# The moving operands of an LSTM's products widened from 8 to 56 columns in the recurrent stage of an eight-part kernel

## What is computed

```
# L2_cond: an LSTM over time; h is (8, 128), Wh is (128, 512)
z = xz_t + prev_h @ Wh
i, f, o = sigmoid(z's first three quarters);  g = tanh(z's last quarter)
next_c = f * prev_c + i * g
next_h = o * tanh(next_c)

# L2_attn: a delta rule, state S (8 batches, 8 heads, 32, 32), on silu(LSTM output @ W_in)
kn = k / (norm(k) + 1e-06)
retrieved = einsum('bhij,bhj->bhi', S, kn)
S = tanh(beta[..., None] * S + (v - retrieved)[..., None] * kn[..., None, :])
Sq = einsum('bhij,bhj->bhi', S, q);  out = Sq * silu(Sq);  x = x + out @ W_out

# L2_cond2: a plain recurrence on the new x
next_h = tanh(prev_h @ Wh + xw_t)
```

## Time and profile before

| | |
|---|---|
| median of 3 runs | 3087.18 us (3081.48 to 3088.09) |
| span of the profiled execution | 3083.1 us |
| mean granted TensorE clock | 0.683 of full speed |
| TensorE (matmul) busy | 86% |
| VectorE / ScalarE / GpSimd busy | 56% / 36% / 24% |

### The profile page before, as it was taken

One profiled execution on the slowest core, in us unless ns is written; L12 is line 12 of the kernel. 1 busy time (PEld: TensorE's weight loads), 2 busy tenths in 40 slices (PEclk: granted clock), 3 DMA queues, 4 the chain that ended last, 5 costly groups with the idle time before them and its releaser, 6 DMA issues. The chain is left out here.

```text
span 3083.1 us, 91254 instructions
## 1 busy us (share of the span) xinstructions
PE 2640.3 (86%) x36709; PEld 1928.4 (63%) x36714; DVE 1738.8 (56%) x7330; ACT 1114.5 (36%) x3986; POOL 750.8 (24%) x1223
## 2 busy tenths in 40 slices
PE   5998878873898889679999999999965878999998
PEld 3556666662555566456777777777543546677774
DVE  3544555555454544456666666666434775576675
ACT  1332333332232223234444444444435433333332
POOL 2110000001110000155555565565523320000000
PEclk9995555555898789555555555555555995799999
DMA  2000000000000000154354455445310000000000
GB/s 86 3 2 2 2 2 3 2 2 37 2 3 1 0 1 0 69 109 85 73 105 86 70 92 91 80 80 105 79 41 1 2 1 2 2 3 2 3 3 15
DMA packets 223764, 103.88 MB, mean 34 GB/s; under 512 B 89472, under 2 KB 220544, under 8 KB 222464
## 3 DMA queue, kind: packets, MB, share of 16 engines
q1 hardware_dynamic: 223360, 98.23, 15.5%
HBM read 89.81 MB, written 8.39 MB: 32 GB/s over the span
## 5 line engine op out<-in xcount | busy, mean ns | idle before, releaser
L641 POOL TENSOR_TENSOR l2r_beta_s<-l2r_state,l2r_beta_f 128x256 f32<-128x256 f32 x512 | 365.9, 736 | 392.3 <-ACT l2r_state L548 374.0
L548 ACT ACTIVATE l2r_state<-l2r_pre 128x256 f32<-128x256 f32 x512 | 191.6, 417 | 267.8 <-DVE l2r_pre L796 267.8
L796 DVE TENSOR_TENSOR l2r_pre<-l2r_o_ps,l2r_beta_s 128x256 f32<-128x256 f32 x512 | 193.7, 420 | 70.8 <-PE l2r_o_ps L439 39.6
L439 PE MATMUL l2r_o_ps<-l2r_rows,l2r_outer 32*128 32x128 f32 x2048 | 207.8, 497 | 13.5 <-DVE l2r_rows L788 13.5
L140 PE MATMUL l0r_bank<-main_x,l0r_wx_half 128*128 128x32 f32 (+2 forms) x480 | 147.4, 407 | 60.5 <-ACT l0r_out_gate L196 60.0
L427 PE MATMUL l2r_d_ps<-l2r_state,l2r_kq 128*32 128x128 f32 x2056 | 176.2, 421 | 13.7 <-ACT l2r_state L548 13.2
L140 PEld LDWEIGHTS l0r_bank<-main_x,l0r_wx_half 128*128 128x128 f32 x480 | 116.2, 304 | 81.7 <-ACT l0r_out_gate L196 79.5
L788 DVE TENSOR_TENSOR l2r_rows<-l2r_d_ps,main_even_layers 128x128 f32<-128x128 f32 x257 | 75.0, 292 | 153.1 <-PE l2r_d_ps L427 151.2
L1785 PEld LDWEIGHTS l3r_bank<-main_x,l3r_wx_half 128*128 128x128 f32 x480 | 96.6, 228 | 90.9 <-issue 46.3
L439 PEld LDWEIGHTS l2r_o_ps<-l2r_rows,l2r_outer 32*128 32x128 f32 x2048 | 132.4, 307 | 33.5 <-DVE l2r_rows L788 28.0
L194 ACT ACTIVATE l0r_gates<-l0r_bank 128x24 f32<-128x24 f32 x256 | 48.9, 191 | 234.4 <-PE l0r_bank L152 234.4
(11 more groups left out here) (582 smaller groups left out, 7320.4 us busy)
## 6 DMA issues: line engine op xcount, KB each, us to landing
l2r_beta_f<-l2r_beta_store SPq DMA_DIRECT2D x256, 256.0 KB, 7.2
main_odd_layers<-in_l SPq DMA_DIRECT2D x1, 4826.5 KB, 15.3
main_odd_layers<-in_l SPq DMA_DIRECT2D x1, 3672.0 KB, 16.4
l2r_v_store<-l2r_v_part SPq DMA_DIRECT2D x32, 96.0 KB, 3.4
l2r_v_rows<-l2r_v_store SPq DMA_DIRECT2D x16, 192.0 KB, 3.2
main_decay<-in_decay SPq DMA_DIRECT2D x1, 3072.0 KB, 10.2
main_even_layers<-in_l SPq DMA_DIRECT2D x1, 2762.5 KB, 10.4
l2r_beta_store<-l2r_beta_tok SPq DMA_DIRECT2D x64, 32.0 KB, 2.0
```

What stands on the lines that cost most here:

```text
L439: last = nc.tensor.matmul(o_ps[:, c, 0:P], outer[chunk_rows(c), n // TC % 2, n % TC, :, :].rearrange("p a b -> p (a b)"), rows[chunk_rows( ...
L548: nc.scalar.activation(state[:, h * 2 * P:(h + 1) * 2 * P], pre[:, h * 2 * P:(h + 1) * 2 * P], ACT.Tanh).then_inc(state_ready[h], 1)
L641: nc.gpsimd.tensor_tensor(beta_s[:, half].rearrange("p (c i) -> p c i", i=N2), state[:, half].rearrange("p (c i) -> p c i", i=N2), beta_f[ ...
L796: nc.vector.tensor_tensor(pre[:, half].rearrange("p (c n) -> p c n", c=2), o_ps[:, 2 * h:2 * h + 2, 0:P], beta_s[:, half].rearrange("p (c ...
```

## The change

The tiles that hold h and its parts become 56 columns wide where they were 8. The 48 new columns are set to zero once, at the stage's start, by four GpSimd memsets that stand before the memsets of `consts_ready`. Each of the 24 LSTM products of a step now moves all 56 columns, and writes 56 PSUM columns from its gate's place on; the 48 further ones get zeros added. The vector operations and the projection read and write the first 8 columns as before. No instruction is taken away or moved, and there is no new wait.

```
+WIDE = 7 * B
...
-        h_ring = mem.sb("h_ring", [P, SLOTS, B])
-        h_rest, h_mid, h_low = mem.sb("h_rest", [P, B]), mem.sb("h_mid", [P, B], BF16), mem.sb("h_low", [P, B], BF16)
+        h_ring = mem.sb("h_ring", [P, SLOTS, WIDE])
+        h_rest, h_mid, h_low = mem.sb("h_rest", [P, WIDE]), mem.sb("h_mid", [P, WIDE], BF16), mem.sb("h_low", [P, WIDE], BF16)
...
-                                last = nc.tensor.matmul(lstm_at(n, g, g + 1), w_part[k][:, g * P:(g + 1) * P],
+                                last = nc.tensor.matmul(lstm_at(n, g, g + WIDE // B), w_part[k][:, g * P:(g + 1) * P],
                                                         h_parts[m], start=False, stop=(m == 2), skip_group_check=True)
...
-                                         h_ring[:, w % 2 * TC:(w % 2 + 1) * TC, :].rearrange("p t b -> p b t"),
+                                         h_ring[:, w % 2 * TC:(w % 2 + 1) * TC, 0:B].rearrange("p t b -> p b t"),
...
+                nc.gpsimd.memset(h_ring[:, :, B:WIDE], 0.0)
+                nc.gpsimd.memset(h_rest[:, B:WIDE], 0.0)
+                nc.gpsimd.memset(h_mid[:, B:WIDE], 0.0)
+                nc.gpsimd.memset(h_low[:, B:WIDE], 0.0)
                 nc.gpsimd.memset(kn_rows[:, :, :], 0.0)
...
-                    nc.vector.tensor_tensor(h_ring[:, n % SLOTS, :], lstm_at(n, 2, 3), tanh_c[:, :],
+                    nc.vector.tensor_tensor(h_ring[:, n % SLOTS, 0:B], lstm_at(n, 2, 3), tanh_c[:, :],
                                             ALU.mult).then_inc(s["h_ready"], 1)
```

More of the change, by code:

```diff
@@ L759, in lstm_h @@
                         dve.wait_ge(s["xin_psum"], n // TC - 1)
-                    nc.vector.tensor_tensor(h_ring[:, n % SLOTS, :], lstm_at(n, 2, 3), tanh_c[:, :],
+                    nc.vector.tensor_tensor(h_ring[:, n % SLOTS, 0:B], lstm_at(n, 2, 3), tanh_c[:, :],
                                             ALU.mult).then_inc(s["h_ready"], 1)
                 def split_alone(n):
-                    h = h_ring[:, n % SLOTS, :]
+                    h = h_ring[:, n % SLOTS, 0:B]
                     dve.wait_ge(s["h_ready"], n + 2)
-                    nc.vector.tensor_tensor(h_rest[:, :], h, high(h), ALU.subtract).then_inc(s["rest_ready"], 1)
+                    nc.vector.tensor_tensor(h_rest[:, 0:B], h, high(h), ALU.subtract).then_inc(s["rest_ready"], 1)
                     dve.wait_ge(s["rest_ready"], n + 2)
-                    nc.vector.tensor_tensor(h_low[:, :], h_rest[:, :], high(h_rest[:, :]), ALU.subtract).then_inc(s["low_ready"], 1)
+                    nc.vector.tensor_tensor(h_low[:, 0:B], h_rest[:, 0:B], high(h_rest[:, 0:B]), ALU.subtract).then_inc(s["low_ready"], 1)
                 def split_h(n):
@@ L776, in split_h @@
                     dve.wait_ge(s["h_psum"], count)
-                    nc.vector.tensor_tensor(rest, lstm_at(n, 3, 4), high(h_ring[:, n % SLOTS, :]),
+                    nc.vector.tensor_tensor(rest, lstm_at(n, 3, 4), high(h_ring[:, n % SLOTS, 0:B]),
                                             ALU.subtract).then_inc(s["rest_psum"], 1)
                     dve.wait_ge(s["rest_psum"], count)
-                    nc.vector.tensor_copy(h_mid[:, :], high(rest)).then_inc(s["mid_h_ready"], 1)
+                    nc.vector.tensor_copy(h_mid[:, 0:B], high(rest)).then_inc(s["mid_h_ready"], 1)
                     dve.wait_ge(s["mid_h_ready"], count)
-                    nc.vector.tensor_tensor(h_low[:, :], rest, h_mid[:, :], ALU.subtract).then_inc(s["low_ready"], 1)
+                    nc.vector.tensor_tensor(h_low[:, 0:B], rest, h_mid[:, 0:B], ALU.subtract).then_inc(s["low_ready"], 1)
                 def masked(n):
@@ L860, in add_out @@
                                             ALU.add).then_inc(s["x_added"], 1)
-                nc.vector.tensor_copy(h_ring[:, SLOTS - 1, :], h0).then_inc(s["h_ready"], 1)
+                nc.vector.tensor_copy(h_ring[:, SLOTS - 1, 0:B], h0).then_inc(s["h_ready"], 1)
                 nc.vector.tensor_copy(r_ring[:, SLOTS - 1, :], h0).then_inc(s["r_ready"], 1)
```

## The result

The changed kernel takes 3171.28 us (median of 4 runs, 3140.52 to 3190.46), the kernel before 3086.8 us beside it: a ratio of 1.0253, 95% interval 1.0202 to 1.0303. It is slower by 2.5%; 2991 us had been forecast, in a range up to 3115. The ratio is taken without the slowest of the four runs, which lies more than 1.5% above the fastest.

The account below looks back on a forecast made before the run. TensorE's order was taken to bound the recurrent steps. -112 us for 224 steps (85% at full clock), +14 and +2 give -96: span 3083.1 becomes 2987, and with 4.1 added, 2991 us; range 2925 to 3115.

Parts of the forecast that it names:

- the forecast of the clock: Recurrent stage: full clock within a wave or two of body 2, for 85% of 224 steps; chance 0.52 for over 80%.
- rival (a): Clock flickers in the recurrent steps; half at full clock gives 3080 us; chance 0.22 still faster, 0.10 slower or near it.
- Rival (b): Clock does not rise, since zeros, or columns as such, don't count: +119 us, 3206 us; chance 0.16.
- The terms at the half clock: 24 widened products cost 0.46 us more a step, weight load hidden: +103 us over 224 steps if the clock stays.
- TensorE's order leaves no slack: In steady recurrent steps the products run straight into `retrieve`, so their whole 0.46 us is paid.
- Alone: The 31 steps where the LSTM runs without the delta rule: +0.46 us each, +14 us.
- Setup: Four new memsets at the stage's start, all on the path: +2 us.
- The term at the full clock: Recurrent steps with LSTM and delta rule: -0.67 us each, 3.03 instead of 3.70, bounds -0.45 and -0.80.
- VectorE is next: At the full clock VectorE's own order limits the recurrent step; nearly all of its 0.62 us waiting goes.
- theory A: Formed after the result: granted clock follows columns streamed through the whole array, zeros included; 56 fall just short.

Follow-up runs that it names:

- The kicked run: The changed kernel with 8 columns in steps 0 to 31 and 20 extra 384-column matmuls after the delta rule's first step: 3154.83 us, ratio 1.0210.
- real data: The changed kernel with the 48 further columns repeating the 8 real columns of h in place of zeros: 3158.62 us, ratio 1.0234.

## Why the prediction was wrong

**The step that failed** is the forecast of the clock: "I take it that the clock rises within a wave or two of body 2 and mostly stays", and in the sum "with 85% of the 224 steps at the full clock". In the profiled execution it was some 6%: 14 steps. That execution is the slowest. If the rest of the program had the full clock for as long in every run, the fastest run (0.707 of 3138.7 us, against 0.684 of 3188.6) had it for some 126 us more in this stage, beside the 48 read in the trace, which would be 20% (an estimate). By that none of the four comes near 85%.

The direction of the mechanism was right (more columns through the whole array do raise the clock: 0.57, 0.90, 0.95, 0.99 for 56, 64, 72, 88), but a step was only said to "come near to that mix" of l3r and, "in its steps with more pieces", to pass it. Near was not enough. And the comparison with l3r was made at the half clock alone. At the full clock an l3r step takes 1.72 us (L1797 starts at 2896.68 and again at 2898.40 in the kernel before), while a step of this stage still takes 3.1, because other engines hold it, so l3r gives TensorE more per microsecond there. Even so l3r lost the clock. The reading that the clock "stayed there" after 2916 leaves out that the same stage had been at 1.0 before 2905 and fell:

```profile
2826.00:2910.00 84.00, 81.72 (x1365) 64.68 (x1364) 57.24 (x319) 30.71 (x155) 1.59 (x3) 0.97 0.01 3
```

The kicked run and the later rises of all four kernels with 56 columns show the same: even at the full clock these steps don't keep it. It was rival (a), flicker, far on the slower side of the 47% at which it turns slower, and that side had a chance of 0.10. Rival (b), 3206 us, is near in time, but its cause is shown wrong: zeros count as data does.

**The terms at the half clock were right.** 0.46 us a step was forecast for the products; 4.18 - 3.70 = 0.48 was measured in three waves, and 0.46 over all 203 steps of the stretch that were at the half clock throughout (4.14, against 3.68 before), with 46.7 ns a product to the tenth and the weights' load hidden. That TensorE's order leaves no slack is shown by VectorE's wait, up by 0.35 us. Alone: 0.46 forecast, 2.5 against 2.0 measured, 13 us in all for the 14. Setup: the timeline of GpSimd in the changed kernel, which answers to the earlier trace rows,

```profile
1243.15 1.37 POOL L733 MEMSET l2r_h_ring<- 128x1536 f32 x1
...
1244.68 0.52 POOL L737 MEMSET l2r_kn_rows<- 128x512 f32 x1
...
1248.95 0.37 PE L359 MATMUL l2r_lstm_psa<-l2r_gate_bf,l2r_bias_t 12*128 12x256 bf16 x1 [6.56 <-POOL l2r_kq L739]
```

has the first old memset 1.5 us behind the first new one, for the 2 forecast.

**The term at the full clock** was a little too large: 3.03 us a step forecast, 3.11 with 64 columns, so -0.59 for -0.67, inside its bounds (with 56 columns the few steps at the full clock took 3.07 to 3.13). That VectorE is next was right in the main: in the run with extra matmuls in the first steps, its waits between 1422.1 and 1875.6 are

```profile
DVE l2r_lstm_psb L762 <- ACT l2r_cand_cell L547: 23.6, 36, 0.7
DVE l2r_rows L800 <- PE l2r_d_ps L433: 9.8, 29, 0.5
DVE l2r_pre L808 <- POOL l2r_beta_s L649: 9.7, 13, 2.2
```

The wait for `retrieve` is down from 65.5 us in 112 steps to 9.8 us in 144, and ScalarE's gates hold it longer than TensorE does. All its waits there come to some 0.3 us a step; the rest of the step is its own order.

So the share of the clock alone accounts for the miss. The forecast's own sum with 6% in place of 85% is 224 x (0.06 x -0.67 + 0.94 x 0.46) + 16 = 104 us. Read from the traces, the 224 steps took 916.2 us for 828.9, 87 more; the LSTM alone 13 and the memsets 1.5 more. That is some 102 us, and the profiled spans differ by 3188.6 - 3083.1 = 105.5; the rest lies outside this stage.

The rule of the Trainium skill (TensorE: Matmul & The Clock Gate, "What's actually happening"), that the gate is opened by how busy TensorE has been, does not agree with these runs if busy is read as the profile's busy time: 710.00 of 710.00 us at 0.50 in one kernel, 84% at 1.00 in another. As work done in the array the runs don't speak against it.

## What to carry to other kernels

In this kernel, padding matmuls to win the clock paid only past a cliff, a width below which the clock stays down. On its near side every padded column is paid at the half clock: 56 columns were 2.5% slower (2.0% with 8 where the LSTM runs alone), while 72, and 8 where the LSTM runs alone, were 2.9% faster. So measure two or three widths, look at the granted clock by stretch rather than at the time alone, and remember that holding the clock is a second condition: it was lost most often just after the steps that give TensorE the least per microsecond, which here are the longest ones at the full clock, and not those with the fewest pieces. A comparison with another stage must therefore be made at the full clock too. And pad where the engine waits anyway: the version with the lowest median put part of the padding ahead of a matmul that waits for VectorE.

## What had not been expected of the hardware

The runs of one kernel near the cliff scatter by far more than usual: 3010 to 3082 us with 64 columns, where the kernel before, measured beside it, spans 3073 to 3087, and the mean granted clock orders them.

The clock also turned at certain steps of the wave. The profiled executions of the four kernels with 56 columns and no extra matmuls in every step (the changed one, real data, the kicked one, 8 while alone) have 14 rises apart from the one made on purpose. All 14 came in steps 2, 4, 11 or 12, each of which has more whole-array columns among its pieces (128) than steps such as 3 and 5. Eight of the 14 falls came in step 9, right after step 8, which at the full clock takes 3.5 us (3.2 in body 3) where steps 7 and 9 take 2.8 to 2.9. That those steps are the cause fits theory A and is not shown by a run of its own, save for steps 0 to 2: with four extra matmuls in each of them instead of two the five falls there were gone.
